# Routing logits from t1 with a token-order norm factor, and a reordered wait ahead of the experts

## The chip, the cores and the metric

The kernel runs on one core of a Trainium2 chip. The metric is device time in microseconds (us): the median of the runs of one kernel, lower is better. The core has five engines with a queue each that work in parallel and meet only at semaphores: TensorE (PE; its weight loads are listed as PEld), VectorE (DVE), ScalarE (ACT), GpSimd (POOL) and SyncE (SP, which here only issues DMAs).

## The reference

Three blocks follow one another on `x` of shape (16, 64, 16, 16): a graph convolution, a selective scan over the 256 tokens of each image (128 channels, 16 states), and a mixture of 8 experts of which each token takes 2. The change lies in the last block, ahead of the experts:

```python
    t = t + _L1_attn_ref(_ln_t(t), ...)                 # t1 below
    t = t + _L1_ffn_ref(_ln_t(t), ...)

    def _ln_t(v, eps=1e-05):
        m = jnp.mean(v, axis=-1, keepdims=True)
        s = jnp.var(v, axis=-1, keepdims=True)
        return (v - m) / jnp.sqrt(s + eps)

    def _L1_ffn_ref(x, Wr, br, ln_g, ln_b, W1, b1, W2, b2):
        xt = x.reshape(N, D)
        logits = xt @ Wr + br
        probs = jax.nn.softmax(logits, axis=-1)
        top_p, top_idx = jax.lax.top_k(probs, TOP_K)
        weights = top_p / top_p.sum(axis=-1, keepdims=True)
        mu = xt.mean(axis=-1, keepdims=True)
        var = ((xt - mu) ** 2).mean(axis=-1, keepdims=True)
        xn = (xt - mu) * jax.lax.rsqrt(var + LN_EPS)
        xe = xn[None, :, :] * ln_g[:, None, :] + ln_b[:, None, :]
        h = jax.nn.gelu(jnp.einsum('end,edh->enh', xe, W1) + b1[:, None, :], approximate=False)
        y = jnp.einsum('enh,ehd->end', h, W2) + b2[:, None, :]
        ...                                             # weighted sum of the two chosen experts
```

So a token is normalized twice: once by `_ln_t`, whose result feeds the router's logits, and once more inside the block for the experts.

## The kernel before

**Tiles.** 128 partitions hold 64 features of two images at a time. Eight groups g = 0 to 7 (two images each, 256 tokens an image, T = 512 columns) are worked off one after another.

**Bodies.** After a prologue (the convolution and the weights' preparation) a loop of eight bodies runs. Body i does the scan of group i, the norm, router and experts of group i-1 (`prev`), and the projections of the groups i+1 (`nxt`) and i+2 (`nxt2`). What is left of group 7 follows as a tail. The order in each engine's queue is written out by hand in one `body` function per engine; every dependency is a semaphore wait (`since` and `so_far` only compute a count).

**DVE** sets out eight slots per body (`dve_slot`): a product into a PSUM ring (L810) and a scan (L816) into a ring of eight `hs` buffers. The scan waits until PE's `pe_sum` (L1117) of the body before has read its buffer. Between the slots stand other pieces: after slot 0 the gate (L837), `rl` (L831) and t1 (L841); after slot 1 the norm and the router (`dve_lnF`, `dve_xn2`, `dve_router1`, `dve_router2`); from slot 4 on one product `mes` (L917) per pair of experts.

**The piece that the change touches**, for group `prev` in body i, in the order of its dependencies:

1. DVE writes t1 (L841). PE centres it: `pe_cenF` (L1194, bank XB). ACT squares it after its decay 9 (`act_lnF1`, L622). PE takes the mean of the squares over the 64 features of each image, which leaves it repeated over partitions: `pe_varF` (L1198). Ahead of `pe_varF` PE runs two dummy matmuls (`pe_warm`, L1296).
2. ACT makes two factors of 128x256 from it, each a Ln and an Exp: `rs2` (L625, L632), one over the root for the router, and `rqs` (L628, L636), for both norms at once, for the experts.
3. DVE writes `tns` = centred t1 times `rs2` (L847). PE's `pe_router` adds the bias by an identity matmul (L1224) and multiplies by the router's weights with `tns` as the stationary operand (L1227): the logits come out with tokens on partitions, in bank XC.
4. DVE writes the experts' input: `xnt2` (L854, two halves) and its rounded copy `X2[0:64]` (L862, two halves), with the first two steps of the router (maximum L867, difference L870) between the halves of L862. ACT takes the exponential (`act_router`, L656) after its decay 13; DVE picks the two experts (L878 to L899).
5. POOL writes the remainder `X2[64:128]` (`pool_x2`, L397; semaphore `xl2`), behind its own product of slot 1.
6. PE waits for `xl2`, runs a dummy matmul, then the C projection of `nxt` (`pe_c`, L1181), then the experts: `pe_f1` (L1265, L1266), ACT's gelu (L680), `pe_f2` (L1280), up to L1280's last and `pe_sum` (L1117).

PE's decay inputs (`pe_spread`, L1209, blocks 8 to 15) stand between these steps, each waiting for ACT's exponential (L617) of two blocks before, since they share two PSUM banks.

In the tail the same steps run for group 7 with nothing else to do; there DVE itself writes the remainder (L1100), and ACT loads the gelu table (L785) after the router's exponential.

Of the kernel before, what the change touches and what calls it, by code (L numbers as in the profile page):

```python
# [26 lines left out]
G = HALF  # L27
# [32 lines left out]
yg po t1 cen2 sq2 var2 ln2 rs2 lnq rq tn xn2 xh2 xl2  # L60
lg lgb m1 dd ex s1 ms1 o1 e2 m2 s2 s2r ms2 o2 den rden num wt wn vhi vlo wtr wtc ld_b2 k_b2 b2r bt_mm bt wb_mm wb
# [9 lines left out]
def build(nc, x, cW1, cb1, Wl, bl, Wr, Wf, bf, cW2, cb2, W_in, b_in, W_conv, b_conv, A_log, W_bc, b_bc,  # L71
# [10 lines left out]
    with ctx:  # L82
# [58 lines left out]
        brs = sb("brs", [128, EXP])  # L141
        W1H = sb("W1H", [128, EXP, FH], f32r)
# [23 lines left out]
        rs2 = sb("rs2s", [128, HW])  # L166
        rqs = sb("rqs", [128, HW])
        tns = sb("tns", [128, HW])
# [450 lines left out]
        def act_lnF1(eng, g):  # L619
            eng.wait_ge(S["cen2"], g + 1)  # L620
            since(eng, "var2", g)
            a_.activation(sq2[:, :], P[:, XB, 0:HW], ACT.Square).then_inc(S["sq2"], 1)  # L622

        def act_rs2(eng, g):
            a_.activation(rs2[:, :], P[:, XB, HW:T], ACT.Ln, bias=epst[:, 0:1]).then_inc(S["ln2"], 1)  # L625
# [4 lines left out]
        def act_rs2_exp(eng, g):  # L630
            eng.wait_ge(S["ln2"], g + 1)
            a_.activation(rs2[:, :], rs2[:, :], ACT.Exp, scale=-0.5).then_inc(S["rs2"], 1)  # L632
# [5 lines left out]
        def act_lnF2(eng, g):  # L638
            eng.wait_ge(S["var2"], g + 1)
            since(eng, "tn", g)  # L640
            since(eng, "xn2", 2 * g)
            since(eng, "xh2", 2 * g)
            if g < G - 1:
                act_rs2(eng, g)
                act_rq(eng, g)
                act_rs2_exp(eng, g)
                act_rq_exp(eng, g)
            else:
                act_rq(eng, g)
                act_rs2(eng, g)  # L650
                act_rq_exp(eng, g)
                act_rs2_exp(eng, g)
# [30 lines left out]
        def _(eng):  # L683
# [22 lines left out]
            def body(i, p, nxt, nxt2, prev):  # L706
# [14 lines left out]
                act_decay(eng, i, 12, 13)  # L721
                if prev is not None:
                    act_router(eng, prev)
                if nxt2 is not None:
                    act_lnA2(eng, nxt2)
# [118 lines left out]
        def dve_lnF(eng, g):  # L844
            eng.wait_ge(S["rs2"], g + 1)
            since(eng, "lg", 2 * g)
            v.tensor_tensor(tns[:, :], P[:, XB, 0:HW], rs2[:, :], ALU.mult).then_inc(S["tn"], 1)  # L847

        def dve_xn2(eng, g, between=None):
# [71 lines left out]
        def _(eng):  # L921
# [127 lines left out]
            def body(i, p, nxt, nxt2, prev):  # L1049
# [17 lines left out]
                if prev is not None:  # L1067
                    dve_lnF(eng, prev)
# [29 lines left out]
            dve_xn2(eng, G - 1, lambda: dve_lnF(eng, G - 1))  # L1098
# [41 lines left out]
        def pe_proj(eng, g):  # L1140
# [5 lines left out]
            eng.wait_ge(S["b1c"], 1)  # L1146
            for h in range(2):
# [151 lines left out]
        def _(eng):  # L1299
# [121 lines left out]
            def body(i, p, nxt, nxt2, prev):  # L1421
# [18 lines left out]
                if prev is not None:  # L1440
                    pe_router(eng, prev)
# [90 lines left out]
```

## Time and profile before

| | us |
|---|---|
| median of 3 runs | 395.5 |
| lowest, highest | 395.02, 399.73 |
| the profiled execution: its own time | 399.41 |
| its span, first to last instruction | 397.7 |

Busy shares of the span: PE 84%, DVE 82%, ACT 70%, POOL 67%. The mean granted TensorE clock is 0.924 of full speed. A busy share is a mean over the prologue, eight bodies and a tail; a row of the timeline gives start, duration, engine, line, output <- inputs, shape and count, and in brackets the idle time of the engine just before, with what ended it.

### The profile page before, as it was taken

What the parts mean: (1) busy time and instruction counts of PE and PEld (TensorE: products, weight loads), DVE (VectorE), ACT (ScalarE), POOL (GpSimd) and SP (SyncE); (2) the same over time, 40 slices, a digit from 0 to 9 for tenths busy, and PEclk for the clock granted to TensorE, in tenths of its full rate; (3) what the DMA queues carried; (4) which work ended last, traced back from release to release, by engine and by line L of the source; (5) the groups of instructions that cost most, each with busy time, mean ns of one, the idle gap of its engine ahead of it and who ended that gap; (6) DMA issues with size and microseconds to landing.
All of it is one profiled execution on the core that took longest, in us unless ns stands there. A gap on an engine that the chain in (4) does not pass through costs nothing. (4 is left out here: it accounts for less than half of the span.)

```text
span 397.7 us, 5508 instructions
## 1 busy us (share of the span) xinstructions
PE 332.3 (84%) x1674; PEld 182.6 (46%) x1674; DVE 325.8 (82%) x428; ACT 277.2 (70%) x465; POOL 267.7 (67%) x255
## 2 busy tenths in 40 slices
PE   0695897487899889987997899789869987999794
PEld 0475445232555345534544464445345524555462
DVE  2777466998899999989999999899999989993411
ACT  1002557589888977899789778997996778661462
POOL 8803503797569967985699589858985895692122
PEclk9996999559899969999999899999987997899698
DMA  7753059899899888859775997589859960000000
GB/s 190 221 118 47 2 140 217 208 222 223 205 218 232 200 214 208 178 129 226 171 176 140 228 210 177 129 188 221 190 126 216 220 163 3 2 2 13 0 0 15
DMA packets 21302, 59.54 MB, mean 150 GB/s; under 512 B 4989, under 2 KB 13337, under 8 KB 15385
## 3 DMA queue, kind: packets, MB, share of 16 engines
q1 hardware_dynamic: 20104, 58.35, 63.6%
q10 hardware_dynamic: 1168, 0.84, 0.9%
q8 instruction: 14, 0.23, 0.3%
q14 instruction: 16, 0.12, 0.1%
HBM read 53.94 MB, written 5.24 MB: 149 GB/s over the span
## 5 line engine op out<-in xcount | busy, mean ns | idle before, releaser
L353 POOL TENSOR_TENSOR hs<-hs,Cs 128x1024 f32<-128x1024 f32 x63 | 149.6, 2377 | 40.3 <-DVE hs L816 39.7
L816 DVE TENSOR_TENSOR_SCAN hs<-av,P 128x1024 f32<-128x1024 f32 x64 | 146.3, 2286 | 6.2 <-PE P L1117 2.9
L680 ACT ACTIVATE hb<-P,b1c 128x512 f32<-128x512 f32 x128 | 81.5, 686 | 21.3 <-PE P L1266 20.9
L810 DVE TENSOR_TENSOR P<-P,ub 128x1024 f32<-128x1024 f32 x62 | 76.0, 1226 | 3.2 <-DMA ub<-u_scratch 0.9
L1280 PE MATMUL P<-hb,W2s 128*64 128x256 f32 x512 | 69.9, 396 | 0.0
L1265 PE MATMUL P<-X,W1H 128*128 128x512 f32 x128 | 61.4, 480 | 2.4 <-ACT hb L680 2.3
L1266 PE MATMUL P<-X,W1L 128*128 128x512 f32 x128 | 53.9, 421 | 0.0
L617 ACT ACTIVATE av<-P,Aneg 128x510 f32<-128x510 f32 x68 | 43.7, 683 | 6.7 <-POOL rl L340 3.5
L1280 PEld LDWEIGHTS P<-hb,W2s 128*64 128x64 f32 x512 | 31.8, 138 | 31.2 <-issue 21.4
L617 ACT ACTIVATE av<-av,Aneg 128x510 f32<-128x510 f32 x60 | 38.3, 707 | 0.3 <-DMA av<-dt_scratch 0.2
L1209 PE MATMUL P<-D,selD 128*128 128x512 f32 x64 | 30.6, 521 | 9.1 <-ACT av L617 6.7
L1265 PEld LDWEIGHTS P<-X,W1H 128*128 128x128 f32 x128 | 26.1, 204 | 21.1 <-ACT hb L680 14.2
L1117 PE MATMUL P<-hs,selS 128*32 128x512 f32 x256 | 30.2, 598 | 2.1 <-POOL hs L353 2.1
L673 ACT ACTIVATE wbs<-P 128x512 f32<-128x512 f32 x32 | 19.1, 598 | 15.3 <-PE P L1245 15.3
L1266 PEld LDWEIGHTS P<-X,W1L 128*128 128x128 f32 x128 | 26.6, 208 | 5.2 <-issue 2.3
L367 POOL TENSOR_TENSOR accs<-accs,mes 128x512 f32<-128x512 f32 x21 | 26.9, 1283 | 2.4 <-DVE mes L917 2.4
L1296 PE MATMUL P<-W1H 128*128 128x512 f32 x47 | 17.2, 464 | 8.2 <-POOL X L397 8.2
L1209 PEld LDWEIGHTS P<-D,selD 128*128 128x128 f32 x64 | 12.7, 205 | 21.7 <-issue 20.4
L917 DVE TENSOR_TENSOR mes<-P,wbs 128x512 f32<-128x512 f32 x28 | 18.7, 667 | 0.2 <-PE P L1280 0.2
L1117 PEld LDWEIGHTS P<-hs,selS 128*32 128x32 f32 x256 | 6.9, 109 | 23.4 <-issue 12.7
L907 DVE SCALAR_TENSOR_TENSOR mes<-P,cols,wbs 128x256 f32<-128x256 f32 x8 | 3.5, 479 | 16.7 <-PE P L1280 8.8
L389 POOL TENSOR_TENSOR D<-dts,D 64x512 fp32r<-64x512 f32 x8 | 10.2, 1274 | 7.8 <-ACT D L600 6.9
(214 smaller groups left out, 522.1 us busy)
## 6 DMA issues: line engine op xcount, KB each, us to landing
ub<-u_scratch SPq DMA_DIRECT2D x31, 1024.0 KB, 10.8
av<-dt_scratch SPq DMA_DIRECT2D x15, 1024.0 KB, 7.1
dt_scratch<-dts SPq DMA_DIRECT2D x7, 256.0 KB, 2.8
u_scratch<-rl SPq DMA_DIRECT2D x7, 256.0 KB, 2.8
av<-in_L_conv_Wr SPq DMA_DIRECT2D x2, 576.0 KB, 7.0
av<-in_L_conv_Wl SPq DMA_DIRECT2D x2, 576.0 KB, 7.6
res<-in_x SPq DMA_DIRECT2D x4, 256.0 KB, 4.6
hb<-in_L_ffn_W SPq DMA_DIRECT2D x2, 512.0 KB, 5.8
```

The lines of the kernel that those rows point to most:

```text
L353: gp.tensor_tensor(hs[:, at, :, :], hs[:, at, :, :], rep(Cs[:, p, :], 1, 2), ALU.mult).then_inc(S["cm"], 1)
L367: done = gp.tensor_tensor(acc[:, :, :], prev, mes[:, at:at + 2, :], ALU.add)
L617: a_.activation(steps, dt_of, ACT.Exp, scale=Aneg[:, m:m + 1]).then_inc(S["aexp"], 1)
L673: a_.activation(wbs[:, 2 * r:2 * r + 2, :].rearrange("p e f -> p (e f)"), P[:, YS, :], ACT.Copy).then_inc(S["wb"], 1)
L680: a_.activation(hb[:, r % 4, :], P[:, (XA, XB)[r % 2], :], ACT.Gelu, bias=b1c[:, r:r + 1]).then_inc(S["gl"], 1)
L810: v.tensor_tensor(ring, rep(P[:, BB, :], 1, 2), ub[:, 2 * n:2 * n + 2, :], ALU.mult).then_inc(S["bm"], 1)
L816: v.tensor_tensor_scan(hs[:, (SLOTS * g + n) % RING].rearrange("p a t -> p (a t)"), av[:, 2 * n:2 * n + 2, :].rearrange("p a t -> p (a t)" ...
L1117: last = pe.matmul(P[32 * q:32 * q + 32, YS, :], selS[:, k, :], hs[:, (SLOTS * g + n) % RING, q % 2, :], start=(k == 0), stop=(k == 3))
L1209: pe.matmul(P[:, (YS, XA)[m % 2], :], selD[:, m - BY_PE[0], :], D2[:, :], start=True, stop=True).then_inc(S["dt_pe"], 1)
L1265: pe.matmul(P[:, bank, :], W1H[:, e, 128 * k:128 * k + 128], X2[:, :], start=True, stop=False)
L1266: pe.matmul(P[:, bank, :], W1L[:, e, 128 * k:128 * k + 128], X2[:, :], start=False, stop=True).then_inc(S["f1"], 1)
L1280: last = pe.matmul(P[64 * h:64 * h + 64, (XC, XD)[pair % 2], HW * (e % 2):HW * (e % 2) + HW], W2s[:, e, k, :], hb[:, r % 4, HW * h:HW * h ...
```

## The change

- The logits are taken from t1 itself: the centring matrix is multiplied into the router's weights once (a matmul in the weights' preparation, copied by DVE to `Wrc`), so `pe_router` needs only t1. It moves up in PE's queue, from behind the spread of block 12 to just ahead of the two dummy matmuls and `pe_varF`. The bias matmul goes.
- A new `pe_vartok` behind `pe_varF` takes the same mean of squares with the squares as the stationary operand: 4 columns with tokens on partitions. `rs2` is made from these: Ln and Exp of 128x4 in the place of 128x256.
- DVE's `tns` goes. `dve_router1` now scales the logits by the factor and adds the bias (two 128x32 operations whose results lie in PSUM) ahead of maximum and difference, and stands as a whole ahead of `dve_xn2`, after a wait for `rs2`.
- ACT runs the experts' Ln first in every body (before only in the tail): Ln, small Ln, Exp, small Exp. Its router exponential moves from behind decay 13 to behind decay 12.
- PE's wait ahead of the experts is for `xh2` (both halves of `X2[0:64]`) in the place of `xl2`, with two dummy matmuls in every body; `pe_c` follows, and `pe_f1` itself waits for `xl2`.
- In the tail the dummy matmuls are spread anew.

```diff
-            a_.activation(rs2[:, :], P[:, XB, HW:T], ACT.Ln, bias=epst[:, 0:1]).then_inc(S["ln2"], 1)
+            eng.wait_ge(S["vt"], g + 1)
+            a_.activation(rv[:, 6], P[:, XC, 4 * EXP:4 * EXP + 4], ACT.Ln, bias=epst[:, 0:1]).then_inc(S["ln2"], 1)
...
-            a_.activation(rs2[:, :], rs2[:, :], ACT.Exp, scale=-0.5).then_inc(S["rs2"], 1)
+            a_.activation(rv[:, 7], rv[:, 6], ACT.Exp, scale=-0.5).then_inc(S["rs2"], 1)
...
-            if g < G - 1:
-                act_rs2(eng, g)
-                act_rq(eng, g)
-                act_rs2_exp(eng, g)
-                act_rq_exp(eng, g)
-            else:
-                act_rq(eng, g)
-                act_rs2(eng, g)
-                act_rq_exp(eng, g)
-                act_rs2_exp(eng, g)
+            act_rq(eng, g)
+            act_rs2(eng, g)
+            act_rq_exp(eng, g)
+            act_rs2_exp(eng, g)
...
-                act_decay(eng, i, 12, 13)
+                act_decay(eng, i, 12)
                 if prev is not None:
                     act_router(eng, prev)
+                act_decay(eng, i, 13)
...
-        def dve_lnF(eng, g):
-            eng.wait_ge(S["rs2"], g + 1)
-            since(eng, "lg", 2 * g)
-            v.tensor_tensor(tns[:, :], P[:, XB, 0:HW], rs2[:, :], ALU.mult).then_inc(S["tn"], 1)
...
         def dve_router1(eng, g):
-            logits = P[:, XC, 0:4 * EXP].rearrange("p (c e) -> p c e", e=EXP)
-            eng.wait_ge(S["lg"], 2 * (g + 1))
+            logits = P[:, XC, 224:224 + 4 * EXP].rearrange("p (c e) -> p c e", e=EXP)
+            eng.wait_ge(S["rs2"], g + 1)
+            eng.wait_ge(S["lg"], g + 1)
+            scaled = P[:, XC, 192:192 + 4 * EXP].rearrange("p (c e) -> p c e", e=EXP)
+            v.tensor_tensor(scaled, P[:, XC, 0:4 * EXP].rearrange("p (c e) -> p c e", e=EXP), rep(rv[:, 7], 2, EXP), ALU.mult).then_inc(S["lm"], 1)
+            eng.wait_ge(S["lm"], 2 * g + 1)
+            v.tensor_tensor(logits, scaled, rep(brs[:, :], 1, 4), ALU.add).then_inc(S["lm"], 1)
+            eng.wait_ge(S["lm"], 2 * g + 2)
             v.tensor_reduce(rv[:, 0], logits, AX, ALU.max).then_inc(S["m1"], 1)
...
-                    dve_lnF(eng, prev)
+                    dve_router1(eng, prev)
                     dve_xn2(eng, prev)
...
+                    v.tensor_copy(Wrc[:, :, :], P[:, XB, 32:32 + 2 * EXP].rearrange("p (h e) -> p h e", e=EXP)).then_inc(S["wrc"], 1)
...
-            dve_xn2(eng, G - 1, lambda: dve_lnF(eng, G - 1))
+            dve_xn2(eng, G - 1)
...
         def pe_router(eng, g):
             eng.wait_ge(S["t1"], g + 1)
-            pe.matmul(P[:, XC, 0:4 * EXP], ident[:, :], rep(brs[:, :], 1, 4), start=True, stop=False).then_inc(S["lgb"], 1)
-            eng.wait_ge(S["tn"], g + 1)
+            eng.wait_ge(S["wrc"], 1)
             for q in range(2):
-                pe.matmul(P[:, XC, 2 * EXP * q:2 * EXP * q + 2 * EXP], tns[:, 128 * q:128 * q + 128],
-                          Wrt[:, :, :].rearrange("p h e -> p (h e)"), start=False, stop=(q == 1)).then_inc(S["lg"], 1)
+                last = pe.matmul(P[:, XC, 2 * EXP * q:2 * EXP * q + 2 * EXP], t1[:, 2 * (g % 2), 128 * q:128 * q + 128],
+                                 Wrc[:, :, :].rearrange("p h e -> p (h e)"), start=True, stop=True)
+            last.then_inc(S["lg"], 1)
+
+        def pe_vartok(eng, g):
+            eng.wait_ge(S["sq2"], g + 1)
+            for q in range(2):
+                last = pe.matmul(P[:, XC, 4 * EXP + 2 * q:4 * EXP + 2 * q + 2], sq2[:, 128 * q:128 * q + 128],
+                                 avg_m[:, 0:128:64], start=True, stop=True)
+            last.then_inc(S["vt"], 1)
...
+            eng.wait_ge(S["ld_dup"], 64)
+            last = pe.matmul(P[:, XB, 2 * EXP * 2:2 * EXP * 2 + 2 * EXP], cen_m[:, :], Wrt[:, :, :].rearrange("p h e -> p (h e)"), start=True, stop=True)
             last.then_inc(S["prep2"], 1)
...
+                    pe_router(eng, prev)
                     pe_warm(eng, 2, XD)
                     pe_varF(eng, prev)
+                    pe_vartok(eng, prev)
...
-                if prev is not None:
-                    pe_router(eng, prev)
                 pe_spread(eng, i, 13)
...
-                    eng.wait_ge(S["xl2"], prev + 1)
-                    pe_warm(eng, 1 if nxt is not None else 2, XB)
+                    eng.wait_ge(S["xh2"], 2 * (prev + 1))
+                    pe_warm(eng, 2, XB)
                 if nxt is not None:
                     pe_c(eng, nxt)
...
             pe_cenF(eng, G - 1, 1)
-            pe_warm(eng, 4)
-            pe_varF(eng, G - 1)
-            pe_warm(eng, 6)
             pe_router(eng, G - 1)
             pe_warm(eng, 3)
+            pe_varF(eng, G - 1)
+            pe_vartok(eng, G - 1)
+            pe_warm(eng, 9)
             pe_pair(eng, G - 1, 0)
```

## Rows read from the trace of the kernel before

**Rows 1.** Windows, bodies 1 to 5: from:to length, busy by engine, PEclk, DMA share.

```profile
131.23:170.37 39.14, 35.54 (x184) 18.77 (x176) 36.43 (x43) 32.83 (x57) 32.58 (x26) 0.91 0.87 202
170.37:208.71 38.34, 34.18 (x196) 18.01 (x192) 36.09 (x42) 34.23 (x60) 29.36 (x24) 1.00 0.75 171
...
sum 191.96, PE 172.49 PEld 91.87 DVE 181.06 ACT 166.35 POOL 151.66; mean PE 34.50 PEld 18.37 DVE 36.21 ACT 33.27 POOL 30.33
```

**Rows 2.** Waits of DVE, 93 to 323 us: total us, times, longest.

```profile
DVE hs L816 <- PE P L1117: 2.9, 3, 1.4
DVE tns L847 <- ACT rs2s L632: 2.8, 3, 1.0
DVE P L810 <- PE P L1173: 0.7, 2, 0.5
```

**Rows 3.** Timeline of DVE, body 4, from slot 1 on: start, us, engine, line.

```profile
214.39 2.29 DVE L816 TENSOR_TENSOR_SCAN hs<-av,P 128x1024 f32<-128x1024 f32 x1
216.65 0.43 DVE L847 TENSOR_TENSOR tns<-P,rs2s 128x256 f32<-128x256 f32 x1
216.99 0.86 DVE L854 TENSOR_TENSOR xnt<-P,rqs 64x256 f32<-64x256 f32 x2
217.89 0.42 DVE L862 TENSOR_TENSOR X<-P,rqs 64x256 fp32r<-64x256 f32 x1
...
218.44 0.19 DVE L870 TENSOR_TENSOR rt<-P,rv 128x32 f32<-128x32 f32 x1
218.66 0.43 DVE L862 TENSOR_TENSOR X<-P,rqs 64x256 fp32r<-64x256 f32 x1
219.12 0.20 DVE L878 SCALAR_TENSOR_TENSOR P<-P,rank 128x32 f32<-128x32 f32 x1
```

**Rows 4.** Timeline of ACT, body 4.

```profile
214.30 0.39 ACT L622 ACTIVATE sq2s<-P 128x256 f32<-128x256 f32 x1
...
215.48 0.47 ACT L625 ACTIVATE rs2s<-P,epst 128x256 f32<-128x256 f32 x1 [0.21 <-PE P L1198]
...
216.21 0.41 ACT L632 ACTIVATE rs2s<-rs2s 128x256 f32<-128x256 f32 x1
```

**Rows 5.** Timeline of PE, body 4.

```profile
214.28 0.63 PE L1296 MATMUL P<-W1H 128*128 128x512 f32 x2
214.75 0.69 PE L1198 MATMUL P<-sq2s,avg_m 128*128 128x256 f32 x2
...
217.13 0.62 PE L1227 MATMUL P<-Wrt,tns 128*128 128x16 f32 x4 [0.66 <-DVE tns L847]
217.65 0.47 PE L1209 MATMUL P<-D,selD 128*128 128x512 f32 x1
...
220.96 0.80 PE L1296 MATMUL P<-W1H 128*128 128x512 f32 x1 [1.41 <-POOL X L397]
...
222.47 1.42 PE L1265 MATMUL P<-X,W1H 128*128 128x512 f32 x1
```

**Rows 6.** Timeline of PE, body 3, the same place at full clock.

```profile
182.99 0.50 PE L1296 MATMUL P<-W1H 128*128 128x512 f32 x1 [0.99 <-POOL X L397]
...
183.78 0.79 PE L1265 MATMUL P<-X,W1H 128*128 128x512 f32 x1
```

**Rows 7.** Timeline of POOL, body 4.

```profile
219.64 1.26 POOL L397 TENSOR_TENSOR X<-xnt,X 64x512 fp32r<-64x512 f32 x1 [0.23 <-POOL hs L353]
```

**Rows 8.** Groups by line and form: count, busy us, mean ns, idle before.

```profile
L692 ACT ACTIVATE gvar<-P,epst 128x8 f32<-128x8 f32 x1 | 0.3, 268 | 4.6 <-PE P L1305 4.6
L694 ACT ACTIVATE grs<-gvar 128x8 f32<-128x8 f32 x1 | 0.2, 209 | 0.0
```

**Rows 9.** Timelines of DVE, PE and ACT at the end of body 7 and in the tail.

```profile
358.20 1.23 DVE L1091 TENSOR_TENSOR hs<-hs,Cs 128x1024 f32<-128x1024 f32 x1
...
361.28 1.06 PE L1117 MATMUL P<-hs,selS 128*32 128x512 f32 x8
...
371.19 1.28 ACT L785 ACT_TABLE_LOAD   x1
```

More of the change, by code:

```diff
@@ L59 @@
 bm scan cm ysum
-yg po t1 cen2 sq2 var2 ln2 rs2 lnq rq tn xn2 xh2 xl2
-lg lgb m1 dd ex s1 ms1 o1 e2 m2 s2 s2r ms2 o2 den rden num wt wn vhi vlo wtr wtc ld_b2 k_b2 b2r bt_mm bt wb_mm wb
+yg po t1 cen2 sq2 var2 ln2 rs2 lnq rq xn2 xh2 xl2
+lg vt lm wrc m1 dd ex s1 ms1 o1 e2 m2 s2 s2r ms2 o2 den rden num wt wn vhi vlo wtr wtc ld_b2 k_b2 b2r bt_mm bt wb_mm wb
 f1 gl f2 me acc out_sem""".split()
@@ L141, in build @@
         brs = sb("brs", [128, EXP])
+        Wrc = sb("Wrc", [128, 2, EXP])
         W1H = sb("W1H", [128, EXP, FH], f32r)
@@ L165, in build @@
         sq2 = sb("sq2s", [128, HW])
-        rs2 = sb("rs2s", [128, HW])
         rqs = sb("rqs", [128, HW])
-        tns = sb("tns", [128, HW])
         xnt2 = sb("xnt2", [64, T])
@@ L621, in act_lnF1 @@
             since(eng, "var2", g)
+            since(eng, "vt", g)
             a_.activation(sq2[:, :], P[:, XB, 0:HW], ACT.Square).then_inc(S["sq2"], 1)
         def act_rs2(eng, g):
-            a_.activation(rs2[:, :], P[:, XB, HW:T], ACT.Ln, bias=epst[:, 0:1]).then_inc(S["ln2"], 1)
+            eng.wait_ge(S["vt"], g + 1)
+            a_.activation(rv[:, 6], P[:, XC, 4 * EXP:4 * EXP + 4], ACT.Ln, bias=epst[:, 0:1]).then_inc(S["ln2"], 1)
         def act_rq(eng, g):
@@ L639, in act_lnF2 @@
             eng.wait_ge(S["var2"], g + 1)
-            since(eng, "tn", g)
+            since(eng, "dd", g)
             since(eng, "xn2", 2 * g)
             since(eng, "xh2", 2 * g)
-            if g < G - 1:
-                act_rs2(eng, g)
-                act_rq(eng, g)
-                act_rs2_exp(eng, g)
-                act_rq_exp(eng, g)
-            else:
-                act_rq(eng, g)
-                act_rs2(eng, g)
-                act_rq_exp(eng, g)
-                act_rs2_exp(eng, g)
+            act_rq(eng, g)
+            act_rs2(eng, g)
+            act_rq_exp(eng, g)
+            act_rs2_exp(eng, g)
         def act_router(eng, g):
@@ L842, in dve_t1, with dve_xn2 @@
                                    in1=res[:, slice(g * HW, g * HW + HW)], op0=ALU.add, op1=ALU.add).then_inc(S["t1"], 1)
-        def dve_lnF(eng, g):
-            eng.wait_ge(S["rs2"], g + 1)
-            since(eng, "lg", 2 * g)
-            v.tensor_tensor(tns[:, :], P[:, XB, 0:HW], rs2[:, :], ALU.mult).then_inc(S["tn"], 1)
-        def dve_xn2(eng, g, between=None):
+        def dve_xn2(eng, g):
             eng.wait_ge(S["rq"], g + 1)
@@ L854, in dve_xn2 @@
                 v.tensor_tensor(xnt2[:, HW * h:HW * h + HW], P[q, XB, 0:HW], rqs[q, :], ALU.mult).then_inc(S["xn2"], 1)
-            if between is not None:
-                between()
             since(eng, "f1", EXP * KC * g)
@@ L859, in dve_xn2 @@
                 q = slice(64 * h, 64 * h + 64)
-                if h == 1 and between is None:
-                    dve_router1(eng, g)
                 v.tensor_tensor(X2[0:64, HW * h:HW * h + HW], P[q, XB, 0:HW], rqs[q, :], ALU.mult).then_inc(S["xh2"], 1)
         def dve_router1(eng, g):
-            logits = P[:, XC, 0:4 * EXP].rearrange("p (c e) -> p c e", e=EXP)
-            eng.wait_ge(S["lg"], 2 * (g + 1))
+            logits = P[:, XC, 224:224 + 4 * EXP].rearrange("p (c e) -> p c e", e=EXP)
[6 more added lines that the diff above has]
+            eng.wait_ge(S["lm"], 2 * g + 2)
             v.tensor_reduce(rv[:, 0], logits, AX, ALU.max).then_inc(S["m1"], 1)
@@ L1223, in pe_router @@
             eng.wait_ge(S["t1"], g + 1)
-            pe.matmul(P[:, XC, 0:4 * EXP], ident[:, :], rep(brs[:, :], 1, 4), start=True, stop=False).then_inc(S["lgb"], 1)
-            eng.wait_ge(S["tn"], g + 1)
+            eng.wait_ge(S["wrc"], 1)
             for q in range(2):
-                pe.matmul(P[:, XC, 2 * EXP * q:2 * EXP * q + 2 * EXP], tns[:, 128 * q:128 * q + 128],
-                          Wrt[:, :, :].rearrange("p h e -> p (h e)"), start=False, stop=(q == 1)).then_inc(S["lg"], 1)
+                last = pe.matmul(P[:, XC, 2 * EXP * q:2 * EXP * q + 2 * EXP], t1[:, 2 * (g % 2), 128 * q:128 * q + 128],
[7 more added lines that the diff above has]
+            last.then_inc(S["vt"], 1)
         def pe_wt(eng, g):
```

## The prediction, made before the changed kernel was run

> **What bounds the kernel now.** I read the windows by body first, then DVE's waits, then the timelines of DVE, ACT and PE around the piece that is changed, and at last the end of body 7. The windows [rows 1] show what to work on: bodies 1 to 5 take 191.96 us, and DVE is busy for 181.06 of them. A body is as long as DVE's own work plus what DVE waits for, so an edit is worth what it does to DVE's queue or to DVE's waits. The waits [rows 2] are few. `tns` waited for the router's factor 2.8 us in three bodies (1, 3 and 5; 1.0 the longest, in body 1). A scan waited 2.9 us in three places for PE to free a buffer of the ring; the longest, 1.4, stands ahead of body 1, so 1.5 lies inside bodies 1 to 5. A product waited 0.7 for the B projection on PE. Together 5.0 us of bodies 1 to 5; without them a body would take (191.96 - 5.0) / 5 = 37.4.
>
> The last two kinds come from an expert phase that PE finishes late, and the windows show when: body 2 has a granted clock of 0.91 and 39.14 us, body 3 one of 1.00 and 38.34 [rows 1]. In body 4 PE stood idle for 1.41 us ahead of its dummy matmul, waiting for POOL's remainder, and the first expert pass behind it took 1.42; in body 3 it stood idle for 0.99 and that pass took 0.79 [rows 5, 6]. So after the longer idle time TensorE ran at the lower of its two levels. The late expert phase delays `pe_sum` (the ring) and ACT's next decays, and with these Square and the factor in the next body, which therefore waits at `tns`. There X2 comes late, so PE's idle time is the short one and the clock holds: slow and late bodies alternate.
>
> In a body that isn't late (body 4) nothing is idle at the piece: slot 1's scan ended at 216.68, `tns` began at 216.65, and the factor had just been made [rows 3, 4]. This balance is the point on which I decide: whatever makes the factor later is a wait of DVE in every body.
>
> **The change part by part.**
>
> *The router ahead of the mean of squares.* `pe_router` now stands between spread 10 and the two dummies. Its four passes took from 217.13 to the next matmul at 217.65, 0.52 [rows 5]. Is there room? Square ended at 214.69 and `pe_varF` began at 214.75, straight behind the dummies [rows 4, 5]. So the dummies only just fill the wait for Square, and the router adds its whole 0.52 to everything behind it: `pe_varF`, spreads 11 to 13, C. The bounds are nothing, if the passes slip into time in which PE is waiting anyway, and 0.52. I take 0.52: that idle time isn't there in body 4. At the old place the router and its wait of 0.66 [rows 5] go, but there PE waits for ACT's decay 11 next, so that frees nothing.
>
> By the Trainium skill (TensorE: Matmul & The Clock Gate, section "Part 2: What happens when you issue a matmul"), weight loads may be pulled ahead of matmuls in flight, while the matmuls stay in order. In the rows above the loads could not go early, since they waited for `tns`; t1 is ready long before. By this rule the passes might cost nearly nothing, and the sum below would come out lower by 6 x 0.52 = 3.1; no run shows it for this place, and I keep the row.
>
> *The token-order mean.* `pe_vartok` is four passes more of the same kind, 0.52 by the same row, behind `pe_varF`. The small Ln that needs them comes behind the experts' Ln of 0.47 [rows 4], which covers them but for 0.05. At the lower clock they would double and show by half a microsecond.
>
> *ACT.* Before: Ln, Ln, Exp to the router's factor, 0.47 + 0.47 + 0.41 = 1.35. Now it is fourth: Ln 0.47, small Ln, Exp 0.41, small Exp. The nearest rows of small ones are 0.27 and 0.21 [rows 8], so 1.36. No difference; 0.1 either way for what overlaps. The exponential of the router now waits for DVE ahead of decay 13, but the difference is out 0.9 after the factor and ACT has decays 11 and 12 and a square to do meanwhile; at nothing.
>
> *DVE.* `tns` (0.34 to its follower) goes, two small operations come, and maximum and difference no longer stand between two products. Before, from `tns` to the choice of the first expert: 216.65 to 219.12 = 2.47. Now four small ones at 0.22 (218.44 to 218.66) and four products at 0.45 (two from 216.99 to 217.89): 2.68 if nothing overlaps, 2.47 if neighbours do, as `tns` and its follower do by 0.1 [rows 3]. I take 2.50: +0.03.
>
> So DVE starts the piece 0.52 later and passes it 0.03 more slowly: **+0.55 per body** (bounds -0.1 and +0.8).
>
> *The wait ahead of the experts.* In body 4's terms the factor is there at 217.17, both halves of X2 0.88 + 1.80 later, at 219.85. PE then runs two dummies (0.47 [rows 5]) and C while POOL makes the remainder: POOL was held until 219.64 by its own product before [rows 7] and now starts about 219.95, done at 221.2. The experts' first pass can start about 221.4, where it started at 222.47 [rows 5]; against body 3, where 0.79 lay between the dummy and the experts [rows 6], at most 0.2 is left. And PE's idle stretch of 1.41 is cut into shorter pieces: one where it waited 0.66 for `tns` and now waits for ACT's decay 11, and short ones ahead of spreads 14 and 15 and of X2; the stretch behind X2 is filled with the dummies and C. I expect the clock to hold in most bodies with `nxt2` work, so the late expert phases and what follows from them go.
>
> *The sum*, against the profiled execution's own 399.41. Lost before in bodies 1 to 5: 5.0. Lost now: body 1 keeps its 1.0 (it is late from body 0, where nothing changes) and adds 0.55, the four others 0.55 each: 3.75. That is -1.25. Body 6: +0.55. Body 0: +0.1 for one small copy; its new matmul is off the path. Body 7: DVE's last product ended at 359.43, but PE came to the last `pe_sum` only at 361.28, behind its own queue [rows 9]. DVE is now there at 359.98, and PE's queue starts at least 0.79 sooner [rows 6], more if the clock holds: between -0.8 and -1.3, I take -1.0. Tail: `tns` (0.43) leaves the way to the router's exponential, two small operations (0.44) join it, and ACT's table load at 371.19 [rows 9] waits for that exponential: 0. Total -1.25 + 0.55 + 0.1 - 1.0 = -1.6: **397.8**.
>
> The median of the runs shown is 395.5, 3.9 below the profiled execution. Bodies 1 to 5 lost 5.0 there, so the quick runs are probably those in which the expert phases didn't start slow. Such a run has nothing to win back: 395.5 + 6 x 0.55 + 0.1 - 1.0 = 397.9. Both ways lead to the same place, so I predict **397.8** for the median. If the 3.9 lies somewhere that the change doesn't touch, it is 395.5 - 1.6 = 393.9.
>
> **The rivals.**
>
> - *The router hides*: nothing is added ahead of the mean, only 0.03 per body. From 397.8 that takes 6 x 0.52 = 3.1: 394.7. For it: t1 is ready early. Against it: passes on both sides of the place without a gap in body 4 [rows 5]. The rule of the Trainium skill named above (TensorE: Matmul & The Clock Gate, Part 2) would lead here.
> - *The clock still falls in some bodies*, since PE still waits in pieces for ACT and then for X2. A slow body costs 39.14 - 37.4 = 1.7 [rows 1]; two of them give 401.2.
> - *Slower beyond doubt*: one mechanism, PE's waits for ACT behind the later mean. If these pieces of idle time make the clock fall in every body, each costs 1.7 more. From 397.8 four such bodies pass 403.4, which is 2% over the median; all six give 408.
> - *Nothing moves*: DVE's wait grows by what the late bodies lose and the end hides the rest: 395.5.
>
> **How the numbers follow.** Forecast (396.3 to 399.3) 0.55; the router hides, or the 3.9 lies elsewhere (393.5 to 395.3) 0.20; nothing moves (395.3 to 396.3) 0.07; some slow bodies (399.3 to 403.4) 0.12; slow in most 0.05; something faster that I don't see 0.01. The range reaches from 393.5 to 400.5. The forecast's own range is 396.3 to 399.3. About 2% is what a measurement of this kernel can tell from no change, with runs from 395.02 to 399.73: faster than 387.6 would need more than all waits of DVE together, 0.02; slower than 403.4, 0.06; within, 0.92.
>
> **What would show it.** In the profile after: DVE's first operation of the router waits for the small Exp in every body, 0.4 to 0.6 us, in place of 0.9 in every second one; `pe_varF` starts half a microsecond behind the end of Square; from DVE's first router operation to the choice of the first expert 2.5; the first expert pass follows POOL's remainder within 0.2, C and dummies ahead of it; granted clock near 1.00 in bodies 2 to 5, and no scan waiting for `pe_sum`; the last `pe_sum` about 1 us sooner after DVE's last product. I am wrong if `pe_varF` starts right behind Square (then it is faster), or if first expert passes of more than 1 us are still there in bodies 2 to 5 (then slower).

## The result, and the profile after

The changed kernel takes **393.85 us** in the median of 20 runs (392.41 to 397.42). The kernel before, run beside it, takes 397.06 in 20 runs (395.02 to 401.2); the three runs shown ahead of the prediction had a median of 395.5. The ratio, which leaves out runs more than 1.5% above the fastest of their kernel, is 0.993, with a 95% interval of 0.9906 to 0.9954 (the two medians give 0.992). That is a small gain, less than the 2% of the bound above, but the interval leaves out 1. The forecast was 397.8, 0.6% slower than 395.5, in a range of 393.5 to 400.5. The time lies in the range; the direction is wrong.

The profiled execution after took 393.65 (before 399.41), its span is 391.9 (before 397.7). The windows of after: bodies 1, 2, 4, 6, 7 and the tail, and then a stretch at the end of body 6 of which the last section speaks (from:to length, busy by engine, PEclk, DMA share):

```profile
93.34:131.00 37.66, 34.68 (x199) 18.28 (x195) 36.15 (x44) 33.22 (x59) 27.81 (x23) 1.00 0.97 219
131.00:168.61 37.61, 34.35 (x195) 17.91 (x187) 36.15 (x43) 32.98 (x58) 30.96 (x25) 1.00 0.90 203
...
206.15:243.68 37.53, 34.25 (x195) 17.91 (x187) 36.15 (x43) 33.02 (x58) 30.96 (x25) 1.00 0.81 186
...
281.25:318.72 37.47, 32.17 (x185) 16.16 (x174) 36.05 (x43) 31.97 (x55) 30.94 (x25) 1.00 0.81 186
318.72:357.10 38.38, 34.06 (x190) 18.12 (x186) 35.47 (x41) 21.63 (x38) 26.79 (x20) 0.96 0.12 29
357.10:391.93 34.83, 25.89 (x136) 15.19 (x136) 9.61 (x30) 15.34 (x28) 8.35 (x15) 0.91 0.04 8
...
312.00:318.70 6.70, 4.42 (x31) 1.16 (x27) 6.65 (x6) 5.67 (x9) 6.49 (x7) 1.00 0.74 168
```

Before, bodies took turns between 39.14 at a clock of 0.91 and 38.34 at 1.00 [rows 1]. After, bodies 1 to 6 all take 37.5 to 37.7, at full clock. Here is the whole difference between the two profiled executions, beside what was predicted:

| part | before | after | difference | predicted |
|---|---|---|---|---|
| up to slot 0's scan of body 1 | 93.23 | 93.34 | +0.11 | +0.1 |
| bodies 1 to 5 | 191.96 | 187.91 | -4.05 | -1.25 |
| body 6 | 37.45 | 37.47 | +0.02 | +0.55 |
| body 7 | 39.77 | 38.38 | -1.39 | -1.0 |
| tail | 35.28 | 34.83 | -0.45 | 0 |
| sum | 397.69 | 391.93 | -5.76 | -1.6 |

The waits of DVE after, 93 to 319 us (total us, times, longest):

```profile
...
DVE hs L812 <- PE P L1111: 1.4, 1, 1.4
DVE P L856 <- ACT rv L633: 1.4, 6, 0.3
```

The scan waits once, ahead of body 1; the products' wait is gone. The factor is waited for in each of the six bodies, for 0.2 to 0.3 us, where before `tns` waited up to 1.0 in every second one [rows 2].

The timelines of body 4 after, PE with its weight loads (PEld), ACT, DVE and POOL; the last two lines are the first gelu of the tail and an operation of PE in body 6, for later sections:

```profile
211.39 0.47 PE L1204 MATMUL P<-D,selD 128*128 128x512 f32 x1
211.59 0.52 PEld L1221 LDWEIGHTS P<-Wrc,t1s 128*128 128x128 f32 x4
211.70 0.51 PE L1221 MATMUL P<-Wrc,t1s 128*128 128x16 f32 x4
212.06 0.71 PE L1298 MATMUL P<-W1H 128*128 128x512 f32 x2
212.60 0.59 PE L1193 MATMUL P<-sq2s,avg_m 128*128 128x256 f32 x2
...
217.92 1.10 PE L1176 MATMUL P<-xc,Wrep 128*128 128x512 f32 x2 [0.27 <-ACT av L616]
218.50 0.75 PE L1267 MATMUL P<-X,W1H 128*128 128x512 f32 x1
...
213.23 0.47 ACT L629 ACTIVATE rqs<-P,eps2t 128x256 f32<-128x256 f32 x1 [0.56 <-PE P L1193]
...
214.06 0.20 ACT L633 ACTIVATE rv<-rv 128x4 f32<-128x4 f32 x1
...
211.80 2.29 DVE L812 TENSOR_TENSOR_SCAN hs<-av,P 128x1024 f32<-128x1024 f32 x1
214.30 0.20 DVE L856 TENSOR_TENSOR P<-P,rv 128x32 f32<-128x32 f32 x1 [0.21 <-ACT rv L633]
...
216.90 0.20 DVE L871 SCALAR_TENSOR_TENSOR P<-P,rank 128x32 f32<-128x32 f32 x1
...
218.24 0.18 DVE L883 TENSOR_TENSOR rt<-rt,rv 128x32 f32<-128x32 f32 x1
...
219.01 1.23 DVE L806 TENSOR_TENSOR P<-P,ub 128x1024 f32<-128x1024 f32 x1
...
217.05 1.28 POOL L396 TENSOR_TENSOR X<-xnt,X 64x512 fp32r<-64x512 f32 x1 [0.23 <-DVE X L849]
...
367.34 1.26 ACT L675 ACTIVATE hb<-P,b1c 128x512 f32<-128x512 f32 x2
...
314.70 0.51 PE L1166 MATMUL P<-ones,bhl 128*128 128x512 f32 x1 [2.28 <-DVE P L806]
```

PE's idle time of 1.41 ahead of the experts [rows 5] has become 0.27 ahead of C, and the first expert pass takes 0.75 in the place of 1.42. It starts 0.17 behind the end of POOL's remainder (217.05 + 1.28 = 218.33).

### The profile page after: what moved, and what is told of

It reads as the page before. It is cut to its first block and busy times, and to the rows that moved or that the text cites. A ratio compares the mean times of both kernels' runs of the same rounds, so it can differ in the third digit from the quotient of the medians.

```text
span 391.9 us, 5577 instructions
## 1 busy us (share of the span) xinstructions
PE 327.0 (83%) x1697; PEld 178.1 (45%) x1697; DVE 321.8 (82%) x437; ACT 273.8 (70%) x465; POOL 267.6 (68%) x255
## 5 line engine op out<-in xcount | busy, mean ns | idle before, releaser
L1267 PE MATMUL P<-X,W1H 128*128 128x512 f32 x128 | 57.1, 446 | 6.3 <-ACT hb L675 4.6
L1268 PE MATMUL P<-X,W1L 128*128 128x512 f32 x128 | 51.6, 403 | 0.0
L1204 PE MATMUL P<-D,selD 128*128 128x512 f32 x64 | 28.7, 489 | 11.5 <-ACT av L616 9.8
L1267 PEld LDWEIGHTS P<-X,W1H 128*128 128x128 f32 x128 | 24.6, 192 | 24.1 <-ACT hb L675 16.3
L1268 PEld LDWEIGHTS P<-X,W1L 128*128 128x128 f32 x128 | 24.9, 194 | 3.5 <-issue 1.0
L1204 PEld LDWEIGHTS P<-D,selD 128*128 128x128 f32 x64 | 11.7, 198 | 25.7 <-issue 25.4
```

Source lines behind the costliest of these rows:

```text
L1204: pe.matmul(P[:, (YS, XA)[m % 2], :], selD[:, m - BY_PE[0], :], D2[:, :], start=True, stop=True).then_inc(S["dt_pe"], 1)
L1267: pe.matmul(P[:, bank, :], W1H[:, e, 128 * k:128 * k + 128], X2[:, :], start=True, stop=False)
L1268: pe.matmul(P[:, bank, :], W1L[:, e, 128 * k:128 * k + 128], X2[:, :], start=False, stop=True).then_inc(S["f1"], 1)
```

## The experiments

Two theories stood against each other. **A:** the moved wait keeps TensorE's clock up, and this is the whole gain; the logits from t1 bring nothing or cost something. **B:** the shorter way to the logits brings a part of the gain by itself. A third question came from the numbers: the piece was to cost 0.55 per body, and hardly any of that is there. Ratios are to the kernel before, run on the same chip.

### The moved wait alone: e1_before_newwait

In the kernel before (where `pe_f1` waits for `xl2` itself, too):

```diff
-                    eng.wait_ge(S["xl2"], prev + 1)
-                    pe_warm(eng, 1 if nxt is not None else 2, XB)
+                    eng.wait_ge(S["xh2"], 2 * (prev + 1))
+                    pe_warm(eng, 2, XB)
```

> The kernel before with one part of the change: PE waits for xh2 ahead of the experts, runs two dummies, then C, and only the experts' first pass waits for xl2. Theory A, the moved wait is the whole gain: bodies 2 to 5 at full clock and 37.5 to 37.6 us each, 393 to 394.5 in all. Theory B, the gain comes from the norm and router piece: the expert phases still start slow in every second body, 396.5 to 397.5.

Measured: 393.77, ratio 0.9922 (0.9883 to 0.996). The windows of bodies 1, 2, 4 and 7 of this kernel:

```profile
94.44:131.73 37.29, 34.37 (x197) 18.06 (x193) 36.07 (x42) 33.32 (x58) 27.69 (x23) 1.00 0.97 223
131.73:169.22 37.49, 33.93 (x193) 17.76 (x185) 36.30 (x43) 33.51 (x58) 30.93 (x25) 1.00 0.87 196
...
207.05:244.53 37.48, 33.97 (x193) 17.78 (x185) 36.38 (x42) 33.11 (x58) 30.91 (x25) 1.00 0.81 182
...
319.46:357.39 37.93, 32.42 (x188) 17.11 (x184) 35.51 (x40) 21.92 (x38) 26.59 (x20) 1.00 0.12 27
```

These few lines bring a gain as large as that of the whole change, with the router's old way untouched. Among DVE's waits in this profile `tns` no longer appears at all: with the expert phases in time, the old factor comes in time too.

### The logits alone: e2_after_oldwait

In the changed kernel:

```diff
-                    eng.wait_ge(S["xh2"], 2 * (prev + 1))
-                    pe_warm(eng, 2, XB)
+                    eng.wait_ge(S["xl2"], prev + 1)
+                    pe_warm(eng, 1 if nxt is not None else 2, XB)
```

> The changed kernel with the old wait ahead of the experts (xl2 first, then one dummy, then C). Theory A: the late expert phases are back in every second body, 396.5 to 398.5. Theory B: it stays at 393.5 to 394.5.

Measured: 399.23, ratio 1.0066 (1.0031 to 1.01), slower than before. The windows of bodies 3 to 5:

```profile
169.44:207.71 38.27, 34.58 (x186) 18.41 (x182) 36.15 (x44) 32.48 (x57) 31.37 (x25) 0.96 0.82 184
207.71:247.06 39.35, 35.13 (x190) 18.68 (x186) 36.24 (x43) 32.87 (x58) 31.37 (x25) 0.96 0.79 182
247.06:285.46 38.40, 34.16 (x198) 18.08 (x194) 36.16 (x44) 33.41 (x59) 30.09 (x25) 1.00 0.79 176
```

and PE's timeline ahead of the experts, two rows of body 2 and two of body 4:

```profile
144.07 0.50 PE L1298 MATMUL P<-W1H 128*128 128x512 f32 x1 [1.32 <-POOL X L396]
...
144.86 0.79 PE L1267 MATMUL P<-X,W1H 128*128 128x512 f32 x1
...
220.83 0.80 PE L1298 MATMUL P<-W1H 128*128 128x512 f32 x1 [1.32 <-POOL X L396]
...
222.34 1.42 PE L1267 MATMUL P<-X,W1H 128*128 128x512 f32 x1
```

Body 4 is the picture of before [rows 5] again: an idle time of 1.32, an expert pass of 1.42, a late body. In body 2 the same idle time was followed by a pass of 0.79, so the idle time alone doesn't tell whether the clock falls. B falls. What the logits cost depends on the wait: under the old one 0.66%, and under the new one nothing that can be measured (393.85 beside 393.77 of e1).

### The clock alone: e3_before_dummies

In the kernel before:

```diff
+                    eng.wait_ge(S["xh2"], 2 * (prev + 1))
+                    pe_warm(eng, 3, XB)
                     eng.wait_ge(S["xl2"], prev + 1)
                     pe_warm(eng, 1 if nxt is not None else 2, XB)
```

> The kernel before with nothing but three dummies more on PE while it waits for POOL's remainder (behind a wait for xh2, ahead of the old wait for xl2, the old dummy and C). If the granted clock alone is what the moved wait gives: full clock in bodies 2 to 5 and 393.5 to 395. If what counts is that C and the dummy are off the way to the experts' first pass: 396 to 397.5, with scans still waiting for pe_sum.

Measured: 393.62, ratio 0.9911 (0.9883 to 0.994). The window of body 4:

```profile
206.18:243.66 37.48, 34.27 (x195) 18.05 (x188) 36.38 (x42) 33.03 (x58) 30.89 (x25) 1.00 0.81 186
```

Nothing is computed sooner or in another order here; three useless matmuls stand in the idle time, and that brings the same. So it is the clock, and not that C is done while POOL works.

### Without the dummies behind X2: e7_no_expert_dummies

In the changed kernel:

```diff
                     eng.wait_ge(S["xh2"], 2 * (prev + 1))
-                    pe_warm(eng, 2, XB)
```

> The changed kernel without the two dummy matmuls behind PE's wait for X2[0:64]; the C projection and the experts follow as before. Theory A (the clock held because the stretch of idle time behind X2 is cut up by dummies and C): without the dummies PE waits about 1.2 us for the remainder around a C of 0.7, the lower clock comes back in some bodies, and the kernel takes 395 to 397. Rival C (C alone, now ahead of the wait for the remainder, is enough to cut the stretch): granted clock 1.00 in bodies 2 to 5 and 393.85 within 0.3.

Measured: 394.03, ratio 0.988 (0.9846 to 0.9914). PE's timeline of body 4:

```profile
216.76 1.10 PE L1176 MATMUL P<-xc,Wrep 128*128 128x512 f32 x2 [0.91 <-ACT av L616]
217.34 0.75 PE L1267 MATMUL P<-X,W1H 128*128 128x512 f32 x1
```

The rival was right: bodies 2 to 5 take 37.51 to 37.54 at a clock of 1.00 without these dummies. C alone, moved ahead of the wait for the remainder, cuts the idle time to 0.91. Either way of filling it will do, C (here) or dummies (e3).

### Without the dummies ahead of the mean: e4_after_nodummy

In the changed kernel:

```diff
                     pe_router(eng, prev)
-                    pe_warm(eng, 2, XD)
                     pe_varF(eng, prev)
```

> The changed kernel without the two dummies behind the router, so that the mean of squares can start when Square is done. If the dummies delay the factor: DVE's wait for it (0.21 to 0.30 us a body) goes and the time falls by 7 x 0.2 = 1.5, to 392.4. If the dummies are needed for the clock: half-clock stretches return and it is 395 or more.

Measured: 393.52, ratio 0.9922 (0.9892 to 0.9953), no different from the changed kernel (in bodies 6 and 7 the clock fell, to 0.95 and 0.91). DVE's wait for the factor is gone, yet body 4 takes 37.47 where it took 37.53. Where the rest of the 0.21 went, DVE's and POOL's timelines of body 4 show:

```profile
216.04 0.42 DVE L883 TENSOR_TENSOR rt<-rt,rv 128x32 f32<-128x32 f32 x1
...
215.15 1.26 POOL L396 TENSOR_TENSOR X<-xnt,X 64x512 fp32r<-64x512 f32 x1 [0.23 <-POOL hs L352]
```

A comparison of 128x32 takes 0.42 where it took 0.18 after the change. It ends at 216.46, and POOL's remainder at 216.41. DVE came earlier, POOL could not (its own product held it), and the comparison now lies beside the remainder. The kernel before shows the same in body 4, the last row being slot 2's product:

```profile
220.47 0.49 DVE L890 TENSOR_TENSOR rt<-rt,rv 128x32 f32<-128x32 f32 x1
...
221.54 1.23 DVE L810 TENSOR_TENSOR P<-P,ub 128x1024 f32<-128x1024 f32 x1
```

It ends at 220.96, and the remainder at 219.64 + 1.26 = 220.90 [rows 7]. The next two runs test whether the one holds up the other.

### POOL's remainder later: e5_pool_late

In the changed kernel, with a tile `late` of 64x128 that nothing reads:

```diff
+            gp.memset(late[:, :], 0.0)
             gp.tensor_tensor(X2[64:128, :], xnt2[:, :], X2[0:64, :], ALU.subtract).then_inc(S["xl2"], 1)
```

> The changed kernel, with one POOL memset of 64x128 ahead of each write of the remainder X2[64:128], so that this write starts some 0.3 to 0.4 us later. DVE's comparison rt6 = (rt5 == second chance), the first router operation with two operands in SBUF, took 0.18 in bodies 1 to 5 after the change, where it started 1.19 to 1.24 behind the start of X2 (X2 takes 1.28), and 0.30 to 0.32 in bodies 6 and 7, where it started 1.0 behind it. Theory P (that operation cannot run while POOL's X2 runs, and ends with it): it starts about 0.9 behind X2 and takes 0.4 to 0.5 in every body, so that a body takes 37.8 in place of 37.55 and the kernel 393.85 + 7 x 0.25 = 395.6. Rival (the operation's length has nothing to do with X2, its 0.49 before was chance): it stays at 0.18, and the kernel at 393.9 within 0.3, since the experts' first pass comes 0.35 later but the clock holds.

Measured: 396.38, ratio 0.996 (0.993 to 0.999). DVE's and POOL's timelines of body 4:

```profile
218.04 0.36 DVE L885 TENSOR_TENSOR rt<-rt,rv 128x32 f32<-128x32 f32 x1
...
217.08 1.27 POOL L398 TENSOR_TENSOR X<-xnt,X 64x512 fp32r<-64x512 f32 x1
```

The memset took only 0.20, so less than planned, but the comparison follows: it starts 0.96 behind the remainder and ends with it (218.40 and 218.35), in the other bodies too. Bodies 2 to 6 take 37.68 to 37.72, 0.1 to 0.2 more each than after the change. The profiled execution took 396.21 against 393.65; most of that difference lies in body 7, which takes 1.6 more at a clock of 0.91. The ratios' intervals of the two kernels overlap, so what the memset costs the whole kernel isn't settled; the bodies show what it does to the comparison.

### Fewer operands in SBUF: e6_nodummy_psum

In e4_after_nodummy; `left` and `second` are 128x32 each in PSUM, bank XC, and `pe_f2` waits for `s2r` in the place of `e2`, since it writes that bank next:

```diff
-            v.scalar_tensor_tensor(out=rt[:, 5], in0=rt[:, 4], scalar=-2.0, in1=chances, op0=ALU.mult, op1=ALU.add).then_inc(S["e2"], 1)
+            v.scalar_tensor_tensor(out=left, in0=rt[:, 4], scalar=-2.0, in1=chances, op0=ALU.mult, op1=ALU.add).then_inc(S["e2"], 1)
...
-            v.tensor_reduce(rv[:, 2], rt[:, 5], AX, ALU.max).then_inc(S["m2"], 1)
+            v.tensor_reduce(rv[:, 2], left, AX, ALU.max).then_inc(S["m2"], 1)
...
-            v.tensor_tensor(rt[:, 6], rt[:, 5], bc(2), ALU.is_equal).then_inc(S["s2"], 1)
+            v.tensor_tensor(second, left, bc(2), ALU.is_equal).then_inc(S["s2"], 1)
...
-            v.tensor_tensor(rt[:, 7], rt[:, 6], rank[:, :, :], ALU.mult).then_inc(S["s2r"], 1)
+            v.tensor_tensor(rt[:, 7], second, rank[:, :, :], ALU.mult).then_inc(S["s2r"], 1)
```

> The changed kernel without the two dummy matmuls ahead of pe_varF (393.52 when it ran alone), and with the chances left and the second choice of the router in PSUM instead of in SBUF, so that the comparison rt6 has one operand in SBUF only. Without the PSUM edit that comparison took 0.37 to 0.66 in bodies 2 to 7, since X2 ran beside it. Theory P (two operands in SBUF collide with POOL's write of X2, one does not): it takes 0.19 in every body, the way from the choice of the first expert to slot 2 falls by 0.15 to 0.25, and the kernel takes 393.5 - 6 x 0.2 = 392.3. Rival (the operation is slow for another reason, or another operation takes over the wait): the way stays as it is, 393.5; if PSUM operands only cost their longer access, up to 394.2.

Measured: 394.32, ratio 0.9889 (0.9856 to 0.9921), on a chip where the kernel before took 398.39. DVE's and POOL's timelines of body 4:

```profile
217.75 0.19 DVE L885 TENSOR_TENSOR P<-P,rv 128x32 f32<-128x32 f32 x1
217.85 0.31 DVE L886 TENSOR_SCALAR rv<-rv 128x4 f32<-128x4 f32 x1
...
216.87 1.27 POOL L396 TENSOR_TENSOR X<-xnt,X 64x512 fp32r<-64x512 f32 x1 [0.23 <-POOL hs L352]
```

The comparison starts inside the remainder, now with one operand in SBUF and its result in PSUM, and takes 0.19. The addition behind it, 0.16 elsewhere, takes over a part: it ends at 218.16, the remainder at 218.14. Bodies 3 to 5 take 37.28 to 37.30 against 37.45 to 37.47 in e4, 0.17 less each, in the expected 0.15 to 0.25. The whole kernel's gain over e4 is not settled: the two ratios' intervals overlap, and the median missed the expected 392.3. In the profiled execution bodies 1 and 7 took 38.49 and 39.52, both at a clock of 0.91.

### Mending what is left: e8_tail and e9_all

First e8_tail, against the changed kernel (the last three pieces are the tail):

```diff
-                    pe_warm(eng, 2, XD)
+                    if nxt2 is None:
+                        pe_warm(eng, 2, XD)
...
-                    pe_warm(eng, 2, XB)
+                    pe_warm(eng, 2 if nxt2 is not None else 4, XB)
...
+            dve_router1(eng, G - 1)
             dve_xn2(eng, G - 1)
...
-            dve_router1(eng, G - 1)
...
-            pe_warm(eng, 9)
+            pe_warm(eng, 17)
```

e9_all has the PSUM edit of e6 as well, and in body 6, ahead of the B projection:

```diff
+                if nxt is not None and nxt2 is None:
+                    pe_warm(eng, 5, XB)
```

> The changed kernel with three places mended: the two dummies ahead of pe_varF only in the bodies without nxt2 (6 and 7); four dummies behind X2 in these two bodies; in the tail DVE's router section ahead of the experts' input, with 17 dummies in place of 9 ahead of the experts. Theory A (the waits named by the trace are what is left): bodies 1 to 5 lose the 0.2 that DVE waits for the factor but gain back 0.1 of X2's collision, -0.5 in all; body 7 keeps its clock, 37.95 in place of 38.38; in the tail gelu's table load is over about 1.0 earlier and the half-clock stretch of 3.4 goes, worth 1.0 to 2.5. Together 393.85 - 0.5 - 0.4 - 1.0 to 2.5 = 390.5 to 392. Rival (the end is bound by the experts' passes on PE, and the clock falls in the tail whatever runs before): the tail stays at 34.8 and the kernel at 393.

> The mended kernel e8_tail with the router's chances left and second choice in PSUM as in e6, and in body 6 five dummy matmuls ahead of the B projection, where PE stood idle for 2.0 and a half-clock stretch began. Theory (the terms add up): bodies 2 to 5 go from 37.47 to 37.3 (4 x 0.17 = 0.7), body 6 from 38.0 to 37.3 where the clock holds, body 7 and the tail stay at 37.87 and 33.6; together 1.4 less than e8_tail, 389.5. Rival (the waits move: POOL's remainder or PE's queue ends last instead): bodies stay at 37.45 and the kernel within 0.4 of e8_tail's 390.9.

Measured: e8 390.9, ratio 0.9822 (0.9781 to 0.9864); e9 391.31, ratio 0.9864 (0.9825 to 0.9903). Both are faster than both kernels (e9 ran on one chip with e10, the changed kernel once more, which took 394.19). The windows of bodies 4, 6, 7 and the tail of e8, and the stretch in which its clock fell:

```profile
204.84:242.28 37.44, 33.93 (x193) 17.52 (x185) 36.28 (x44) 32.99 (x58) 30.93 (x25) 1.00 0.82 185
...
279.74:317.74 38.00, 32.99 (x179) 16.77 (x172) 36.07 (x43) 31.67 (x55) 31.47 (x25) 0.96 0.81 184
317.74:355.61 37.87, 34.23 (x200) 17.80 (x192) 35.36 (x41) 21.50 (x38) 26.14 (x20) 1.00 0.13 29
355.61:389.23 33.62, 26.43 (x144) 16.16 (x144) 9.52 (x30) 15.36 (x28) 8.54 (x15) 0.99 0.04 8
...
313.40:316.80 3.40, 3.40 (x11) 0.88 (x14) 3.40 (x3) 3.10 (x6) 3.40 (x5) 0.50 0.45 96
```

The first gelu of the tail in ACT's timeline of e8:

```profile
365.08 1.27 ACT L675 ACTIVATE hb<-P,b1c 128x512 f32<-128x512 f32 x2 [1.70 <-PE P L1268]
```

The windows of bodies 4, 6 and 7 of e9:

```profile
204.86:242.16 37.30, 33.94 (x193) 17.57 (x185) 36.14 (x43) 32.98 (x58) 30.91 (x25) 1.00 0.83 187
...
279.46:316.79 37.33, 34.30 (x188) 18.47 (x180) 35.93 (x42) 30.77 (x54) 30.88 (x25) 0.95 0.83 187
316.79:355.22 38.43, 35.46 (x200) 18.58 (x190) 35.38 (x41) 22.70 (x40) 26.88 (x20) 0.96 0.12 29
```

The tail falls by 1.2, from 34.83 to 33.62. The first gelu starts 9.47 behind the tail's start (365.08 less 355.61) in place of 10.24 (367.34 less 357.10), because the table is loaded while DVE still works on the experts' input, and the clock is 0.99 in place of 0.91. In e9 the bodies fall to 37.30 as expected, but what e8 kept in body 7 (37.87) is lost to a clock of 0.96 (38.43). So the terms of the bodies add up and those of the clock don't; the expected 389.5 wasn't reached, and no median below that of e8.

### The changed kernel once more: e10_after_again

> The changed kernel itself, unaltered, as a second sample of its time beside e9_all on one chip: 0.993 of the kernel before, bodies 1 to 6 at 37.5 to 37.7 with a granted clock of 1.00, if the profile of after is typical of it; if half-clock stretches come back in bodies 2 to 6, the bodies of the first profile were luck, and the gain is not safe.

Measured: 394.19, ratio 0.993 (0.9901 to 0.9959). Bodies 1 to 6 take 37.48 to 37.66, all at a clock of 1.00: the first profile is typical.

## Why the prediction was wrong, point by point

- **Where the time lay: right.** The late expert phases come from the lower clock behind the idle time ahead of them, and the moved wait removes them. e1 and e3 show it, each by a different edit. Granted clock 1.00 in bodies 2 to 5, the first expert pass 0.17 behind the remainder, no scan waiting inside these bodies: all as forecast. Body 7, for which -1.0 was forecast, gave -1.39, and the tail, forecast at 0, gave -0.45 at a clock of 0.91 in place of 0.87.
- **The router ahead of the mean, +0.52: too high, and partly for the reason that the rival gave.** From its first pass to the dummies it takes 0.36 (211.70 to 212.06), and the dummies up to `pe_varF` take 0.54 in place of 0.47 [rows 5]: +0.43. The four weight loads still take 0.52, but the first begins at 211.59, under spread 10, which began at 211.39; so 0.36 is left of them. The Trainium skill (TensorE: Matmul & The Clock Gate, section "Part 2: What happens when you issue a matmul") has weight loads pulled ahead of matmuls in flight. The trace agrees in kind, with 0.16 of the 0.52 hidden; "nearly nothing" it is not.
- **`pe_vartok` hidden, ACT at nothing: right, with a small gain.** `pe_varF` to ACT's first Ln fell from 0.73 to 0.63, and from there to the end of the factor from 1.14 to 1.03. In both rows each operation starts about 0.1 before its neighbour ends; four operations have three such overlaps where three had two, and the sum of 1.36 had counted none. With the 0.43 that is +0.22. In body 4 DVE's first router operation starts 0.21 behind the end of the scan, where `tns` started 0.03 ahead of it [rows 3]: +0.24. So the balance on which the prediction decided was right: what makes the factor later is a wait in every body. It was 0.2 to 0.3, not 0.5.
- **DVE's own part, +0.03: this step failed, and with it the +0.55 per body.** Up to the choice of the first expert it takes 2.60 in place of 2.47, +0.13. But I counted only as far as that choice. From there to slot 2 it takes 2.11 (216.90 to 219.01) in place of 2.42 (219.12 to 221.54): -0.31, the comparison that POOL's remainder had held up. The remainder starts at the same place in the body (10.90 behind the start of slot 0's scan, before 10.93), but DVE reaches the comparison 0.33 later (12.09, before 11.76), when the remainder is nearly done. The sum is 0.24 + 0.13 - 0.31 = **+0.06** in body 4, in place of +0.55, and just that lies between 37.53 here and 37.48 in e1, whose router is the old one. e4, e5 and e6 show the term from three sides. In before the comparison took 0.31, 0.49, 0.52 and 0.41 in bodies 2, 4, 6 and 7, and 0.18 in bodies 1, 3 and 5, where DVE had waited for the factor; in e1, where nothing waits for the factor, it took 0.39 to 0.69 in bodies 2 to 7. So the old router pays this in nearly every body that isn't late. Bodies 1 to 5 take 37.58 in the mean, 0.18 more than the 37.4 of the prediction but only 0.07 more than in e1 (37.51).
- **"Body 1 is late from body 0", 1.0 kept: wrong.** It was a half-clock stretch inside body 1. This window of before shows it, at 0.50, the lower of the two levels (1.2 of 2.4 GHz):

```profile
98.10:101.50 3.40, 3.40 (x9) 2.59 (x9) 2.85 (x2) 2.28 (x6) 2.81 (x3) 0.50 0.98 212
```

  After, body 1 has a clock of 1.00, but the change didn't bring that. In e1 and e3, which run the instructions of before up to there, body 1 has a clock of 1.00 too and takes 37.29 and 37.30 in place of 38.00; in e6 such a stretch is back. So about 0.7 of the 5.76 between the two profiled executions is luck. With body 1 the account of bodies 1 to 5 closes: -1.25 forecast, less 1.0, less 5 x (0.55 - 0.18) = 1.85, is -4.1; measured -4.05. That is bookkeeping and no proof, since the 0.18 comes from the same windows.
- **"The quick runs have nothing to win back": this is what turned the direction.** I took 395.5, the median of three runs, for a run without late bodies. Over 20 runs the kernel before takes 397.06, and e1 and e3 take 3.3 to 3.4 off the median by PE's idle time alone. So the common run does lose time there. The quick ones ran at a low clock, too: over all later runs of the kernel before, those under 395.5 have a mean granted clock of 0.931 to 0.936, and all runs of the changed kernel 0.944 to 0.962. Where in a quick run the clock fell, no trace shows. The rows of the profiled execution were worth more than a story about runs whose trace I didn't have.

Nearest in time came the prediction's other sum, 393.9. That is luck: its 395.5 lies 1.6 below the median of 20 runs, and its gain of 1.6 is 1.6 short of the 3.2 between the medians, so two errors cancel. The rival at 394.7 named one term of three: the passes hid 0.16 of their 0.52, the way from `pe_varF` to the factor gave 0.2 and the comparison 0.3. What stays open is why the clock falls where it does in bodies 6, 7 and the tail.

## What to carry to other kernels

Where PE waits ahead of a long run of matmuls, look first for work that needs less (a projection, or dummies), and put it into the wait: here that alone was worth 0.8 to 0.9%, as much as the whole change. Cost a change up to the next operation of the bounding engine that hasn't moved, not up to the last one that was edited; a neighbour that comes earlier or later may give back what the edit takes. And compare with the execution whose rows one has read, rather than with three times whose traces one doesn't have.

## What the runs showed of the hardware

- **VectorE held up by GpSimd.** A comparison of 128x32 with both operands in SBUF takes 0.18 alone. Where it starts while POOL's subtraction of 64x512 runs, it ends with that: 0.49 in body 4 of before, 0.42 in e4, 0.36 in e5. With one operand and the result in PSUM it took 0.19 at the same place (e6), but the addition of 128x4 behind it, with a single operand in SBUF, was then held instead: 0.31 in place of 0.16. The Trainium skill (SBUF — State Buffer, section "SBUF: two separate sides") says that VectorE and GpSimd share a pair of ports as an exclusive lock for the whole instruction, and that VectorE needs it with two inputs in SBUF beside a GpSimd instruction that reads SBUF. The trace agrees for the comparison: the ends lie within 0.06 of each other in the three rows that were held up. I had not looked for it, since the busy shares show a held-up operation as work.
- **The clock isn't decided by one idle time alone.** In body 6 of after PE stood idle for 2.28 ahead of the B projection, and the granted clock stayed 1.00 (312.00 to 318.70). In e8 PE stood idle for 1.98 at the same place, and the clock was 0.50 from 313.40 on:

```profile
313.21 0.65 PE L1166 MATMUL P<-ones,bhl 128*128 128x512 f32 x1 [1.98 <-DVE P L806]
```

  Ahead of the experts it is the same: in before the clock held behind idle times of 0.99 and 1.00 (bodies 1, 3 and 5) and fell around those of 1.21 to 1.41 (bodies 2, 4, 6 and 7), but in e2 the first expert pass took 0.79 in bodies 2 and 5 and 1.42 in bodies 1 and 4, all four behind 1.31 to 1.32. No run here shows what tells these apart.
